# A turned context: a picking matmul of 36 columns in place of a transpose of 128

## What is computed

```python
scores = jnp.einsum('bhqd,bhkd->bhqk', q, k) / math.sqrt(hd)
attn = jax.nn.softmax(scores, axis=-1)
ctx = jnp.einsum('bhqk,bhkd->bhqd', attn, v)
ctx = ctx.transpose(0, 2, 1, 3).reshape(B, S, D)
return ctx @ Wo.T
```

## Time and profile before

| | |
|---|---|
| Three timed runs | 1075.86, 1080.92, 1081.12 us; median 1080.92 us |
| Span of the profiled execution | 1115.6 us (no other time of this execution is recorded) |
| TensorE busy | 905.9 us, 81% of the span |
| VectorE busy | 817.5 us, 73% |
| ScalarE busy | 726.9 us, 65% |
| GpSimd busy | 346.0 us, 31% |
| Mean granted TensorE clock | 0.896 of full speed |

### The profile page before, as it was taken

One profiled execution on the slowest core, in us unless ns is written; L12 is line 12 of the kernel. 1 busy time (PEld: TensorE's weight loads), 2 busy tenths in 40 slices (PEclk: granted clock), 3 DMA queues, 4 the chain that ended last, 5 costly groups with the idle time before them and its releaser, 6 DMA issues. The chain is left out here.

```text
span 1115.6 us, 17986 instructions
## 1 busy us (share of the span) xinstructions
PE 905.9 (81%) x5934; PEld 362.1 (32%) x5934; DVE 817.5 (73%) x1141; ACT 726.9 (65%) x1580; POOL 346.0 (31%) x598
## 2 busy tenths in 40 slices
PE   2354459999999989898988988898898769869982
PEld 1222012222222222221212221222222168859972
DVE  3886988999999988877998798789871025613366
ACT  0043018888888878777887877788788646526651
POOL 1333000000000262043035205223323327666883
PEclk9667559999999989988998998899999779968997
DMA  4054430404402000071000000100000012112353
GB/s 123 0 196 179 162 129 1 149 16 152 158 25 105 30 2 29 23 198 49 1 30 6 25 30 25 44 1 30 1 1 13 27 44 61 54 60 68 102 146 111
DMA packets 57049, 72.69 MB, mean 65 GB/s; under 512 B 9504, under 2 KB 37664, under 8 KB 56960
## 3 DMA queue, kind: packets, MB, share of 16 engines
q1 hardware_dynamic: 52416, 62.21, 17.3%
q0 software_dynamic: 4544, 9.35, 2.4%
HBM read 30.08 MB, written 41.06 MB: 64 GB/s over the span
## 5 line engine op out<-in xcount | busy, mean ns | idle before, releaser
L860 DVE TENSOR_REDUCE half_max<-ps_max 128x2 f32<-128x1024 f32 x512 | 601.7, 1219 | 90.7 <-PE ps_max L676 71.6
L791 ACT ACTIVATE probs<-ps_scores 128x512 f32<-128x512 f32 x1024 | 540.1, 603 | 112.2 <-PE ps_scores L697 99.0
L710 PE MATMUL ps_ctx<-probs,v_grp 128*32 128x512 f32 x2048 | 286.5, 633 | 0.7 <-ACT probs L791 0.7
L697 PE MATMUL ps_scores<-q_set,k_set 51*128 51x512 bf16 x1024 | 261.2, 398 | 27.1 <-ACT probs L791 16.0
L676 PE MATMUL ps_max<-k_set,q_set 48*128 48x512 bf16 x1024 | 195.9, 409 | 70.4 <-DVE half_max L860 57.2
L697 PEld LDWEIGHTS ps_scores<-q_set,k_set 51*128 51x128 bf16 x1024 | 68.6, 94 | 347.9 <-ACT probs L791 304.1
L613 POOL TENSOR_TENSOR ctx<-turned,inv_sum 128x128 f32<-128x128 f32 x32 | 13.1, 410 | 375.7 <-DVE inv_sum L887 375.2
L1527 ACT ACTIVATE hid<-ps_up,w_tile 128x128 f32<-128x128 f32 x312 | 89.3, 370 | 58.5 <-PE ps_up L1693 53.3
L676 PEld LDWEIGHTS ps_max<-k_set,q_set 48*128 48x128 bf16 x1024 | 51.0, 96 | 177.8 <-DVE half_max L860 156.5
L1492 POOL DMA_INDIRECT y_rows<-y,y_to x78 | 91.6, 1174 | 48.9 <-DVE y L1564 32.9
L1564 DVE TENSOR_TENSOR y<-ps_down,w_tile 128x128 f32<-128x128 f32 x78 | 22.8, 292 | 104.0 <-PE ps_down L1703 58.9
(11 more groups left out here) (197 smaller groups left out, 658.0 us busy)
## 6 DMA issues: line engine op xcount, KB each, us to landing
slots<-zero_rows SPq DMA_DIRECT2D x43, 387.0 KB, 6.0
q_terms<-parts SPq DMA_DIRECT2D x24, 256.0 KB, 2.5
k_terms<-parts SPq DMA_DIRECT2D x24, 256.0 KB, 3.2
q_set<-q_terms SPq DMA_DIRECT2D x32, 192.0 KB
k_set<-k_terms SPq DMA_DIRECT2D x32, 192.0 KB
slots_in<-slots SPq DMA_DIRECT2D x78, 64.5 KB
rows<-y_rows SPq DMA_DIRECT2D x16, 256.0 KB
w_all<-in_we SPq DMA_DIRECT2D x1, 2048.0 KB
```

What stands on the lines that cost most here:

```text
L697: pe.matmul(bank[:], k_set[g % SETS][operand, u, tile * P:(tile + 1) * P], q_set[g % SETS][operand, u, c * BANK:(c + 1) * BANK], start=Tru ...
L710: ins = pe.matmul(ps_ctx[32 * head:32 * head + 32, :], v_grp[g % 2][:, tile, head, :], probs[:, s % RING, head, :], start=tile == 0, stop= ...
L791: act.activation(probs[:, s % RING, place, :], ps_scores[n % BANKS_S][:], ACT.Exp, scale=float(HD) ** -0.5).then_inc(slot_taken, 1)
L860: dve.reduce_max(half_max[g % 2][:, c, 2 * u:2 * u + 2, tile], ps_max[n % 2][:].rearrange("p (r n) -> p r n", r=2), axis=AX.X).then_inc(ma ...
```

## The change

The four transposes of `turn_ctx` become four float32 matmuls. The stationary operand is the same block of `ctx_t`, the moving operand is a new matrix `pick` of 128 rows and 36 columns (`PICKED` = 9 columns for each of the 4 heads), with a one where row 32 x head + column is to be picked. The result has 36 columns for each of the four blocks, 144 in all in place of 512, packed one behind the other. ScalarE copies these 144 columns; `turned` shrinks to 4 x 4 x 9 values a partition; the inversion and the product read the same values at another stride. `pick` is made by GpSimd ahead of the identities.

```diff
+PICKED = HD + 1
...
             pool.wait_ge(pool_done, own.more(3))
+            pool.memset(k["pick"][:], 0.0).then_inc(pool_done, 1)
+            pool.wait_ge(pool_done, own.more())
+            for head in range(GH):
+                pool.affine_select(out=k["pick"][:, head], in_=k["pick"][:, head], compare_op=ALU.not_equal, fill=1.0,
+                                   base=-32 * head, pattern=[[-1, PICKED]], channel_multiplier=1).then_inc(ident_ready, 1)
             for m in ("ident", "ident16"):
...
-            pe.wait_ge(ident_ready, 2)
+            pe.wait_ge(ident_ready, GH + 2)
...
-        turned = [sb(f"turned{i}", [P, BANK]) for i in range(2)]
+        turned = [sb(f"turned{i}", [P, 4, GH, PICKED]) for i in range(2)]
...
-                view = turned[chunk % 2][:].rearrange("p (t h c) -> p t h c", h=GH, c=32)
-                pool.tensor_tensor(out, view[:, :, :, 0:HD],
+                pool.tensor_tensor(out, turned[chunk % 2][:, :, :, 0:HD],
...
+                pick = k["pick"][:].rearrange("p h c -> p (h c)")
                 for i in range(4):
-                    ins = pe.transpose(bank[:, i * P:(i + 1) * P], ctx_t[chunk % 2][:, i * P:(i + 1) * P],
-                                       k["ident"][:])
+                    ins = pe.matmul(bank[:, i * GH * PICKED:(i + 1) * GH * PICKED], ctx_t[chunk % 2][:, i * P:(i + 1) * P],
+                                    pick, start=True, stop=True)
                 ins.then_inc(slot_ready, 1)
...
-                act.copy(turned[chunk % 2][:], ps_scores[n % BANKS_S][:]).then_inc(slot_taken, 1)
+                act.copy(turned[chunk % 2][:].rearrange("p t h c -> p (t h c)"),
+                         ps_scores[n % BANKS_S][:, 0:4 * GH * PICKED]).then_inc(slot_taken, 1)
...
-                view = turned[chunk % 2][:].rearrange("p (t c) -> p t c", c=32)
+                view = turned[chunk % 2][:].rearrange("p t h c -> p (t h) c")
```

More of the change, by code:

```diff
@@ L119, in build @@
             "ident16": sb("ident16", [P, P], BF16),
+            "pick": sb("pick", [P, GH, PICKED]),
             "rsqrt_exp": sb("rsqrt_exp", [P, NT]),
```

## The result

The changed kernel takes 1086.49 us (median of 4 runs, 1082.50 to 1088.11), the kernel before 1079.55 us in the same comparison (4 runs, 1075.86 to 1081.12): a ratio of 1.0066, 95% interval 1.0039 to 1.0092. By the ratio the change costs 7.1 us, by its interval 4.2 to 9.9 us. The forecast was 1090 us, +9.2, slower.

A forecast was written before the change was run, and what follows sets the result against it. Behind a turn, TensorE and a late PSUM bank, 0.17 us apart, were taken to bound the kernel. Terms 6.0 + 1.3 + 0.8 + 0.6 + 0.5 = +9.2 us gave 1090 us, own range 1088 to 1093, outer ends 1081 to 1098.

The forecast's parts named there:

- half absorbed case: Attention stage: half of the 24 ordinary turns' loss vanishes in shorter waits for VectorE's maxima; 1087 us.
- The turn on TensorE: Attention stage: eight instructions replace four; the slot grows from 0.59 to 1.01 us, 0.42 us longer.
- that rival: Turn on TensorE gets no longer, since columns and not instructions set its time; 1080.6 us, chance 0.04.
- What the bank hides: Behind a turn, an existing 0.17 us wait for a PSUM bank hides that much of the 0.42 us growth.
- clean turn: One of 24 attention-stage turns with a 2.88 us step; each costs 0.25 us more, 6.0 us together.
- place 2: Score matmul behind a turn, started 0.17 us after place 1 because its bank was late; afterwards both start together.
- No absorption: Denies the rival that VectorE's maxima become the bound in attention steps; 1084 us if all absorbed, chance 0.13.
- The copy: ScalarE's 32 copies shorten by some 0.3 us each, costed at nothing for 31; rival: 1072 us, chance 0.07.
- The clock: Rival: steadier TensorE work keeps full clock in three half-clock stretches touching turns; 10 us back, 1080 us, chance 0.08.
- turns with logits: Three attention-stage turns sharing their step with a routing matmul; nothing hides the growth, 3 x 0.42 = 1.3 us.
- one turn at half clock, three odd ones: Attention stage: one turn in a half-clock stretch costs 0.8 us; three beside other waits 0.2 each, 0.6 us.
- last turn: Ends the attention stage at half clock: 0.8 us longer turn less 0.3 us shorter copy, 0.5 us.

The follow-up runs named there:

- first profile: The kernel before, no edit: the profiled execution from which the prediction was read; span 1115.6 us.
- second profile: The kernel before, no edit, profiled again; span 1074.0 us, 1075.78 us in one run.
- moved place: Against the kernel before, four transposes and their copy moved to right behind the context matmuls: ratio 1.0045 with the short copy, 1.0082 with the long.

## Why the prediction was right

The kernel became slower by the mechanism of the forecast, by 7.1 us in place of 9.2. The time of 1086.49 us lies 1.5 us under the forecast's own range (1088 to 1093). By the time alone the half absorbed case (1087) would fit as well; the steps decide between them.

*The turn on TensorE.* Predicted 1.01 us from the neighbours with 8 and 128 columns, measured 1.01; eight instructions for four matmuls, 256 in all, as predicted. Matmuls of 128 columns (1.09) and eight transposes (1.02) show why: fewer columns hardly shorten it, twice the instructions nearly double it. By the sentence of the Trainium skill ("TensorE: Matmul & The Clock Gate", "Part 2: What happens when you issue a matmul") that throughput is N cycles, taken alone, the turn would have become shorter; the runs disagree at these sizes, and that rival (1080.6 us) falls. The Trainium skill's page "Perfetto Trace Analysis", "Transposes", prefers a transpose to a matmul, since it skips the arithmetic; the sign agrees (0.59 against 1.01 us), but eight transposes at 1.02 us show that what is saved here is instructions, four in place of eight.

*What the bank hides.* Predicted 0.17 of 0.42 us, so 0.25 per clean turn and a step of 3.13 us (3.11 to 3.21). Measured: the two scores start together behind each of the 26 turns, and the row of five, six and eight transposes turns at the predicted point. But 3.13 holds for nine of the 26; the other 17 are 3.08 to 3.10, just under the band, because 0.20 or 0.22 us were hidden there. The prediction read the 0.17 in one row and took the 24 clean turns to be alike "in rows that differ by 0.01 us"; that holds for the length of the step, but in the first profile too place 2 is 0.20 to 0.22 us late behind 17 of the 24. That the sum comes out at 6.0 is partly luck: two more turns, at 0.02 us less each.

*No absorption.* The prediction gave 0.13 to VectorE taking up half or more. The step right behind a turn is the same within 0.01 us in all 31 cases, and VectorE waits 0.25 us longer behind a turn. This rival falls.

*The copy.* Predicted at nothing for 31 of 32, and it was nothing, in both directions (short copy alone: 1.0006; long copy with the matmuls: every step as after). ScalarE's busy time fell by 6.1 us, not 9: the last 0.1 us of a long copy lay under the exp behind it (0.58 us long, 0.48 to the next start), and counted once.

*The clock.* 0.98 in the stage before and after; this rival falls.

*The terms that were off*, against the execution without long steps:

| term | predicted | measured |
|---|---|---|
| clean turns | 24 x 0.25 = 6.0 | 26 x 0.23 = 6.0 |
| turns with logits | 3 x 0.42 = 1.3 | 3 x 0.50 = 1.5 |
| one turn at half clock, three odd ones | 0.8 + 0.6 | two cost 0, two are clean |
| last turn | 0.5 | 0.12 |
| sum | 9.2 | 7.6 |

The overshoot of about 1.6 us has two sources. The half clock of the last turn and of one more, and a third turn in a long step, were taken from one profiled execution of 1115.6 us and carried over to runs of 1080 us. The last turn shows it plainly: 0.63 us in the second profile, 1.08 in the first. (The factor of 1.9 for the half clock is also more than the two durations that it is taken from: 1.08 / 0.66 = 1.6.) The other two odd turns are no accident: they are those of the last group, where TensorE comes to the turn so early that the bank, 0.48 us late in the second profile, hides all of the 0.42 us; 0.2 us each was a guess where the reading used for the clean turns would have given next to nothing. The logits term is too small for another reason (last section).

## What to carry to other kernels

Where a slot of work sits in a ring of buffers, read from the row behind it how far the two limits lie apart, the engine that comes late and the buffer that comes late: a shorter slot gains nothing below that hinge, and a longer one costs only what goes beyond it. The lag differs from one turn to the next (0.17 to 0.48 us here), so read it at each. Four float32 transposes made into four float32 matmuls are eight instructions in place of four, and at 8 to 128 columns their number sets the time; fewer columns don't pay that back. A shorter copy is worth something only where its engine is what the loop waits for; here it was so in the moved place (0.17 us a turn) and not in its own.

## What the runs showed of the hardware

In these runs a slot of float32 matmuls on TensorE goes by its loads of the stationary block. In the step with a turn and logits, the loads (PEld) before (second profile) and after:

```profile
444.54 0.42 PEld L729 LDWEIGHTS ps_scores<-ident,ctx_t 128*128 128x128 f32 x4 [0.23 <-issue]
444.93 0.97 PEld L1343 LDWEIGHTS ps_scores<-rw,router_act_attend 128*128 128x128 f32 x8
445.92 0.10 PEld L697 LDWEIGHTS ps_scores<-q_set,k_set 51*128 51x128 bf16 x2
```

```profile
448.83 0.97 PEld L736 LDWEIGHTS ps_scores<-pick,ctx_t 128*128 128x128 f32 x8 [0.23 <-issue]
449.71 0.97 PEld L1351 LDWEIGHTS ps_scores<-rw,router_act_attend 128*128 128x128 f32 x8
450.71 0.10 PEld L703 LDWEIGHTS ps_scores<-q_set,k_set 51*128 51x128 bf16 x2
```

From the turn's first load to that of the logits it is 0.39 us with four transposes and 0.88 to 0.89 with eight picking matmuls; with eight matmuls of 128 columns it is 0.89 too. From there to the scores it is 0.99 to 1.00 us in all three. So where another float32 slot follows, the turn costs its four more loads, 0.50 us, and its columns cost nothing. This is why the three steps with logits grew by 0.50 us, where the prediction took the 0.42 of a clean turn, and why they are 4.00 us long with 36 and with 128 columns. In a clean turn the columns count once, at its end: from the turn's last load to the scores it is 0.24 us with 36 columns and 0.32 with 128. The stationary block has 128 columns in all these cases; what a narrower one would give, no run shows.

The other thing is the copy out of PSUM: 0.28 us for 144 columns and 0.58 for 512. An exp whose scores are done starts before the copy ahead of it ends: 0.48 us after the start of a long copy, and 0.16 us after that of a short one in the last group of the run with the short copy alone (847.51 and 847.67 us). The short copy so frees ScalarE some 0.3 us earlier, as its duration says. In the other turns the exp starts 0.32 us after it, and that is a wait for the scores: in the kernel after they are done at 230.86 + 0.39 = 231.25 us, and the exp starts at 231.29.
